# Transformer block, one core: another order of the pieces that stand beside the pairs of heads

## The reference

```python
x = x + attention(layernorm(x))      # softclamp 50*tanh(s/50), causal, softmax, projection Wo
n = layernorm(x)
shared = gelu(n @ sw1 + sb1) @ sw2 + sb2
probs = softmax(n @ gate_w + gate_b);  topk_p, topk_i = top_k(probs, 2)
routed = sum over the two chosen e: topk_p[e] * (gelu(n @ w1[e] + b1[e]) @ w2[e] + b2[e])
x = x + routed + shared
```

## Time and profile before

| | |
|---|---|
| median of 3 runs | 2223.99 us (2222.87 to 2224.55) |
| profiled execution, own time | 2222.78 us |
| its span | 2221.1 us |
| busy: TensorE, VectorE, ScalarE, GpSimd | 1953.5, 1495.0, 1419.2, 1003.5 us |
| mean granted clock of TensorE | 0.958 |
| one sequence in the steady part | 112.75 us |
| second stage, from 1835 us on | some 386 us |

### The profile page before, as it was taken

The page is one execution under the profiler, slowest core; times in us unless marked ns, Lnnn a source line. Parts: engine busy times, 40 slices in busy tenths (PEclk is TensorE's granted clock), DMA queues, the critical chain, the costliest instruction groups (busy, mean ns, idle before and its releaser), DMA issues.

```text
span 2221.1 us, 39929 instructions
## 1 busy us (share of the span) xinstructions
PE 1953.5 (88%) x14653; PEld 1525.6 (69%) x14653; DVE 1495.0 (67%) x2803; ACT 1419.2 (64%) x2170; POOL 1003.5 (45%) x1195
## 2 busy tenths in 40 slices
PE   6889898989898989898989989898989876699898
PEld 4666676766666767676666767576767654699898
DVE  5467767676767686767676767676767685566565
ACT  6768575767676766767685857676767651344444
POOL 3434545453535353535353536353535442444344
PEclk9999999999999999999999999999999987799999
DMA  3000101010101010101010101010100012665564
GB/s 123 1 10 12 38 10 39 10 39 10 39 10 39 11 39 11 39 11 39 11 39 10 39 10 39 10 39 11 39 11 30 11 39 98 211 186 173 164 183 142
DMA packets 73665, 112.51 MB, mean 51 GB/s; under 512 B 9715, under 2 KB 52218, under 8 KB 73476
## 3 DMA queue, kind: packets, MB, share of 16 engines
q1 hardware_dynamic: 58468, 67.86, 10.5%
q0 software_dynamic: 15008, 42.10, 5.1%
HBM read 63.10 MB, written 48.65 MB: 50 GB/s over the span
## 4 chain that ended last, share of the span: by engine, by line
PE 43%; DVE 28%; ACT 21%; issue 7%; DMA 1%; POOL 0%; another core or an unknown queue 0%; POOLq 0%; DVEq 0%; SPq 0%; ACTq 0%
PE ring L1188 6%; ACT prob L590 5%; ACT prob L584 5%; PE bank_o L1230 5%; DVE norm L795 4%; DVE q_lo L784 4%; PE ring L1209 3%; DVE kT L779 3%; PE ring L1195 3%; PE ring L1214 3%; ACT kT L597 2%; ACT qT L607 2%; ACT qT L601 2%; DVE oTl L809 2%; PE ring L1136 2%
## 5 line engine op out<-in xcount | busy, mean ns | idle before, releaser
L508 POOL TENSOR_SCALAR_AFFINE_SELECT prob<-prob 128x256 f32<-128x256 f32 x512 | 219.2, 443 | 683.1 <-ACT prob L590 683.0
L584 ACT ACTIVATE prob<-ring 128x1024 f32<-128x1024 f32 (+1 forms) x384 | 328.1, 877 | 269.2 <-PE ring L1214 265.1
L779 DVE TENSOR_TENSOR kT<-ring,kT 64x512 fp32r<-64x512 f32 x256 | 176.3, 688 | 414.6 <-ACT kT L597 336.6
L1230 PE MATMUL bank_o<-prob,v 128*32 128x512 f32 (+3 forms) x4096 | 327.4, 463 | 103.3 <-DVE weighed L800 85.0
L520 POOL TENSOR_TENSOR key_sum<-prob 128x768 f32<-128x768 f32 x128 | 236.5, 1848 | 261.8 <-PE bank_d L1244 252.1
L590 ACT ACTIVATE prob<-prob 128x1024 f32<-128x1024 f32 (+1 forms) x384 | 344.0, 914 | 5.2
L1230 PEld LDWEIGHTS bank_o<-prob,v 128*32 128x32 f32 x4096 | 122.0, 115 | 284.3 <-issue 188.3
L1209 PE MATMUL ring<-qT,kT 128*128 128x256 f32 (+3 forms) x1024 | 244.2, 341 | 79.5 <-ACT qT L607 23.5
L1209 PEld LDWEIGHTS ring<-qT,kT 128*128 128x128 f32 x1024 | 168.9, 192 | 156.7 <-DVE q_lo L784 37.0
L795 DVE RECIPROCAL norm<-bank_d 128x512 f32<-128x512 f32 x64 | 214.7, 3355 | 26.5 <-PE bank_d L1244 25.5
L1214 PE MATMUL ring<-q_lo,kT 128*128 128x256 f32 (+3 forms) x1024 | 229.0, 325 | 0.0
(11 more groups left out here) (224 smaller groups left out, 4665.0 us busy)
## 6 DMA issues: line engine op xcount, KB each, us to landing
xin<-first SPq DMA_DIRECT2D x71, 257.0 KB
xin<-second SPq DMA_DIRECT2D x71, 129.0 KB
xin<-base SPq DMA_DIRECT2D x71, 128.0 KB, 2.1
x_next<-in_x SPq DMA_DIRECT2D x16, 512.0 KB, 4.6
x_res<-in_x SPq DMA_DIRECT2D x16, 512.0 KB, 3.8
raw_e<-in_w SPq DMA_DIRECT2D x4, 1024.0 KB, 6.8
first<-pad SPq DMA_DIRECT2D x9, 257.0 KB, 8.7
second<-pad SPq DMA_DIRECT2D x9, 129.0 KB, 8.1
```

The source lines that it names most:

```text
L508: last = nc.gpsimd.affine_select(out=diag, in_=diag, compare_op=ALU.is_ge, fill=0.0, base=0, pattern=[[0, 2], [1, P]], channel_multiplier=-1)
L584: nc.scalar.activation(probs[p % PROBS][u][:, :, :], slot[:, :, 0:UNIT_COLS[u]], ACT.Tanh, scale=SCALE / SOFTCLAMP).then_inc(act_emptied, 1)
L779: last = nc.vector.tensor_tensor(kT[head_rows[1 - h], h, :], slot[r, 1, :], kT[r, h, :].bitcast(F32), ALU.subtract)
L1230: last = pe.matmul(bank_o[h * QD:(h + 1) * QD, j * P:N], v[:, j, f:f + QD], probs[(2 * quad + h // 2) % PROBS][u][:, h % 2, at:at + N - j ...
```

## The change

It gives pieces of a sequence other pairs to stand beside, on all engines, and computes the same.

- First layer norm of the next sequence: from pair 0 to pair 1, behind the weighing and splitting of the previous sequence's pair 7.
- Value projections: three at pair 1 and one at pair 2, instead of two and two. The output projection of the previous sequence's pair 6 goes from between the first two to behind the last one; that of pair 7 goes from pair 2 to pair 3.
- `add_attention` and the second layer norm: from pair 2 to pair 3. `turn2`: from 3 to 4. `gate`: from 4 to 5. `turn_logits`: from 4 to 5. `hidden` stays at 5, now directly behind `gate`. `choose` and `split_hidden`: from 5 to 6, behind `empty_turned1`. `count_earlier`: from the end of 6 to 7, ahead of `shared_out`.
- `empty_pos` is cut out of `place_tokens`; it stands with the rest behind `empty_qk` of pair 7, and `place_tokens` now follows `add_shared`, where it stood ahead of the weighing.
- Transfers of rows: `send_second` from pair 7 to pair 0 of the sequence after, `send_first` from pair 0 to pair 1, both behind `sum_keys`.

```diff
--- before.py
+++ after.py
@@ -90,7 +90,7 @@
             elif i + 1 < NSEQ:
                 units += [("qk", i + 1, 0, 0)]
             if i >= 1 and p in FFN_UNITS:
-                units += [(FFN_UNITS[p], i - 1, 0, 0)]
+                units += [(kind, i - 1, 0, 0) for kind in FFN_UNITS[p]]
             if i + 1 < NSEQ and p == 6:
                 units += [("turn1", i + 1, 0, 0)]
             if p in V_UNITS:
@@ -102,10 +102,10 @@
 
 
 UNIT_ORDER = (2, 0, 1)
-V_UNITS = {1: (0, 1), 2: (2, 3)}
-
-FFN_UNITS = {3: "turn2", 4: "gate", 5: "hidden", 7: "out"}
-LATE_UNITS = {4: "logits", 6: "pos"}
+V_UNITS = {1: (0, 1, 2), 2: (3,)}
+
+FFN_UNITS = {4: ("turn2",), 5: ("gate", "hidden"), 7: ("pos", "out")}
+LATE_UNITS = {5: "logits"}
 LAST_UNITS = ["turn2", "gate", "logits", "hidden", "pos", "out"]
 RING = ring_plan()
 AT = {unit: n for n, unit in enumerate(RING)}
@@ -529,12 +529,13 @@
             pool.wait_ge(const_ready, 2)
             for i in range(NSEQ):
                 for p in range(PAIRS):
+                    mask(i, p)
+                    sum_keys(i, p)
                     if p == 0 and i >= 2:
+                        send_second(i - 2)
+                    if p == 1 and i >= 2:
                         send_first(i - 2)
-                    mask(i, p)
-                    if p == PAIRS - 1 and i >= 1:
-                        send_second(i - 1)
-                    sum_keys(i, p)
+            send_second(NSEQ - 2)
             send_first(NSEQ - 2)
             pool.wait_ge(projected, NSEQ * PAIRS)
             clear_pad()
@@ -645,13 +646,13 @@
                     clamp(i, p, 0)
                     clamp(i, p, 1)
                     exponentiate(i, p, 0)
-                    if i >= 1 and p == 5:
+                    if i >= 1 and p == 6:
                         exp_gate(i - 1)
                     if p >= 3:
                         exponentiate(i, p, 1)
 
                     def meanwhile():
-                        if p == 3 and i >= 1:
+                        if p == 4 and i >= 1:
                             copy_x2_hi(i - 1)
                         if p == 6 and i + 1 < NSEQ:
                             copy_xn_hi(i + 1)
@@ -883,23 +884,25 @@
                 last.then_inc(chosen_ready, 1)
 
 
-            def place_tokens(i):
-
+            def empty_pos(i):
                 n = AT["pos", i, 0, 0]
                 slot = ring[n % 2]
-                step = [0]
-
-                def then(ins):
-                    step[0] += 1
-                    ins.then_inc(slot_steps, 1)
-                    dve.wait_ge(slot_steps, i * SLOT_STEPS + step[0])
-
                 ahead = slot[:, 0, 0:K * NT * E].rearrange("p (k t e) -> p k t e", k=K, t=NT)
                 totals = slot[:, 1, 0:K * NT * E].rearrange("p (k t e) -> p k t e", k=K, t=NT)
                 dve.wait_ge(ring_full, n + 1)
                 nc.vector.tensor_copy(place[:, :, :, :], ahead)
                 nc.vector.tensor_copy(totals_of[:, :, :, :], totals).then_inc(dve_emptied, 1)
-                dve.wait_ge(dve_emptied, EMPTIED[n][1])
+
+            def place_tokens(i):
+
+                step = [0]
+
+                def then(ins):
+                    step[0] += 1
+                    ins.then_inc(slot_steps, 1)
+                    dve.wait_ge(slot_steps, i * SLOT_STEPS + step[0])
+
+                dve.wait_ge(dve_emptied, EMPTIED[AT["pos", i, 0, 0]][1])
                 for t in range(NT):
                     then(nc.vector.tensor_tensor(taken[:, :, t + 1, :], taken[:, :, t, :], totals_of[:, :, t, :],
                                                  ALU.add))
@@ -980,11 +983,8 @@
                     chunk = (i, p - 3) if p >= 3 else (i - 1, p + 5)
                     if p == 2 or chunk[0] < 0:
                         chunk = None
-                    if i >= 1:
-                        if p == 5:
-                            empty_logits(i - 1)
-                        if p == 7:
-                            place_tokens(i - 1)
+                    if i >= 1 and p == 6:
+                        empty_logits(i - 1)
                     if i == 0 and p == 3:
                         dve.wait_ge(idle_padded, 16 * 3)
                     if chunk is not None:
@@ -1001,34 +1001,36 @@
                         split_lo(3 + p)
                         if p == 1:
                             split_lo(5)
-                    if p == 0 and i + 1 < NSEQ:
+                    if p == 1 and i >= 1:
+                        weigh_values(i - 1, PAIRS - 1)
+                        split_values(i - 1, PAIRS - 1)
+                    if p == 1 and i + 1 < NSEQ:
                         dve.wait_ge(xnext_loaded, 16 * (i + 2))
                         layernorm_stats(1, x_next)
                         layernorm_guess(1, i + 1)
                         layernorm_newton(1, i + 1)
                         layernorm_apply(1, i + 1, x_next, x_next, xn_ready)
-                    if p == 1 and i >= 1:
-                        weigh_values(i - 1, PAIRS - 1)
-                        split_values(i - 1, PAIRS - 1)
-                    if i == NSEQ - 1 and p in (3, 4, 5, 6):
-                        prepare_bias(p - 3)
+                    if p == 6 and i + 1 < NSEQ:
+                        empty_turned1(i + 1)
+                    if i == NSEQ - 1 and p in (4, 5, 6, 7):
+                        prepare_bias(p - 4)
                     if i >= 1:
-                        if p == 2:
+                        if p == 3:
                             add_attention(i - 1)
                             layernorm_guess(2, i - 1)
                             layernorm_newton(2, i - 1)
                             normalise_rows(i - 1)
-                        if p == 3:
+                        if p == 4:
                             empty_turned2(i - 1)
-                        if p == 4:
+                        if p == 5:
                             empty_gate(i - 1)
-                        if p == 5:
+                        if p == 6:
                             choose(i - 1)
                             split_hidden(i - 1)
                         if p == 7:
+                            empty_pos(i - 1)
                             add_shared(i - 1)
-                    if p == 6 and i + 1 < NSEQ:
-                        empty_turned1(i + 1)
+                            place_tokens(i - 1)
 
             last_i = NSEQ - 1
             for c in range(PAIRS - 3, PAIRS):
@@ -1043,6 +1045,7 @@
             empty_logits(last_i)
             choose(last_i)
             split_hidden(last_i)
+            empty_pos(last_i)
             place_tokens(last_i)
             add_shared(last_i)
 
@@ -1315,30 +1318,27 @@
                 pe.matmul(slot[:, 0, 0:K * NT * E], earlier[:, :], flags, start=True, stop=True)
                 pe.matmul(slot[:, 1, 0:K * NT * E], ones_r[:, :], flags, start=True, stop=True).then_inc(ring_full, 1)
 
-            FFN = {2: turn2, 3: gate, 4: hidden, 5: turn_logits, 6: shared_out, 7: count_earlier}
-
             pe.wait_ge(const_ready, 2)
             turn1(0)
             pe.wait_ge(xn_hi, 1)
             project_qk(0, 0, (lo_split, 1), (lo_split, 2))
-            MIDDLE = {3: turn2, 4: gate, 5: hidden, 7: shared_out}
-            LATE = {4: turn_logits, 6: count_earlier}
+            MIDDLE = {4: (turn2,), 5: (gate, hidden), 7: (count_earlier, shared_out)}
+            LATE = {5: turn_logits}
             for i in range(NSEQ):
                 for p in range(PAIRS):
                     for u in UNIT_ORDER:
                         scores(i, p, u)
                     if p >= 4:
                         project_out(i, p - 4)
-                    elif i >= 1 and p < 2:
+                    elif i >= 1 and p != 2:
                         project_out(i - 1, p + 4)
-                    elif i >= 1 and p == 2:
-                        project_out(i - 1, PAIRS - 1)
                     if p + 1 < PAIRS:
                         project_qk(i, p + 1)
                     elif i + 1 < NSEQ:
                         project_qk(i + 1, 0)
                     if i >= 1 and p in MIDDLE:
-                        MIDDLE[p](i - 1)
+                        for piece in MIDDLE[p]:
+                            piece(i - 1)
                     if i + 1 < NSEQ and p == 6:
                         turn1(i + 1)
                     if p == 1:
@@ -1346,13 +1346,10 @@
                             values(i - 1, PAIRS - 1)
                         else:
                             pe.wait_ge(lo_split, 3)
-                        project_v(i, 0)
-                        if i >= 1:
-                            project_out(i - 1, PAIRS - 2)
-                        project_v(i, 1)
-                    if p == 2:
-                        project_v(i, 2)
-                        project_v(i, 3)
+                    for t in V_UNITS.get(p, ()):
+                        project_v(i, t)
+                    if p == 2 and i >= 1:
```

(9 more changed lines are left out.)

## The result

The kernel after takes 2408.89 us (median of 4 runs, 2407.67 to 2412.61) against 2224.27 us before: a ratio of 1.083, with a 95% interval of 1.0815 to 1.0847. It is slower, as forecast, but by 185 us and not by 109: the time lies above the range. Its profiled execution took 2412.61 us.

The account below looks back on a forecast made before the run. TensorE was taken to set the pace at 112.75 us a sequence. Pair terms summed to 121.3, 8.55 more; 14 x 8.55 = 120, less the ends, gave +109, or 2333 us; range 2285 to 2362, eight in ten.

Parts of the forecast that it names:

- the two waits: TensorE idle before pair 3's first scores, about 6.7 us, and before `shared_out` at pair 7, some 7 us.
- the step of 5.93 us: TensorE's gap before the values of pair 7 at pair 1, forecast to go with 1.4 us of slow clock.
- the 5 to 8 us that the prediction named as their sign: Profile sign: TensorE idles this long before pair 3's first scores and before `shared_out`, both released by L784.
- its own last sign of being wrong: Prediction is wrong if the layer norm at pair 2 is as slow as GpSimd's adds can make it.
- so I take 6.0: Pair 2: 6.0 us for the first layer norm, GpSimd waiting for denominators until it is about half done.
- the upper end I had kept (8.04): Pair 2: slowest layer norm duration read before, kept for the range as +2.0 us on the 6.0.
- nearer 8: Pair 2: layer norm duration in us if small steps each wait out one GpSimd add, by the skill's rule.
- The term of 5.45: Pair 7: us for `choose` and `split_hidden` on VectorE, within the 13.6 us chain before `shared_out`.
- 3.43+1.8: Pair 7: shared output 3.43 us, plus 1.8 us for the clock after some 7 us idle.
- 11 back: First and last sequences: -4 us in sequence 0 and -7 us in the last, against 120 us added.
- costed at nothing: Row transfers behind `sum_keys`: hidden in GpSimd's waits; up to 5 us a sequence if that cover were gone.
- Rival 3: Both waits, VectorE further behind: norm 8.0, clocks 2.1 each, transfers partly uncovered; 11.5 us a sequence, about 2373 us; chance 0.07.

Follow-up runs that it names:

- two single edits: Kernel after, output projection of pair 6 back behind the first value projection: 2288.74 us; kernel after, `empty_qk` ahead of the reciprocal at pair 7: 2323.52 us.
- the norm alone: Kernel before with only the first layer norm moved from pair 0 to pair 1, behind weighing and split of pair 7: 2113.28 us.
- both edits: Kernel after with the output projection of pair 6 back and `empty_qk` ahead of the reciprocal at pair 7: 2202.75 us, ratio 0.991 to before.

## Why the prediction was right and wrong

The direction and the mechanism of the two waits held: the step of 5.93 us goes, and both new waits come at the places, by the releasers and with the causes that were named. The two single edits and their sum show them to be separate, and the norm alone shows that it was not the norm's place that was bad. Both waits are longer than the 5 to 8 us that the prediction named as their sign (8.79 and 8.49), and its own last sign of being wrong came true: the norm is as slow at its new place as GpSimd's adds can make it. Of the pairs, 0, 1, 3, 4 with 5, and 6 came within 0.3 us. `hidden` waits 1.34 us (1.5 forecast), the slot of the turned rows 0.91 (1.2), the split more than 15.

The size was wrong. In the spans, 189.8 us came where 109 were forecast; of the 81 missed, 64 lie in the 14 sequences and 17 at the ends. **Pair 2** took 23.1 us and not 20.4. The term that failed is "so I take 6.0" for the layer norm: it measured 8.52. I reasoned that GpSimd would stand still for its first half; it did, but the small steps of the second half were held up all the more, and the upper end I had kept (8.04) was too low also. The first scores unit then took 1.02 us and not 0.6, at the low clock that the sum had put into pair 3. The rule of the Trainium skill that I had put beside it, "SBUF — State Buffer", "Who interferes with whom", would have made it "nearer 8" and was the better guide: the small steps end with GpSimd's adds, and short adds bring 5.59. **Pair 7** took 23.8 and not 21.6. The term of 5.45 for `choose` and `split_hidden` measured 6.88, for the same reason: I had read it at a place where the adds had nearly ended. And `shared_out` with its slow clock took 5.84 us and not 3.43+1.8. The norm and the choice, 2.52 and 1.43 us above their terms, make 55 us in 14 sequences, most of the 64. That cutting the adds short gave 75 us, about the whole miss, is partly chance: the choice then took 4.94, less than its term, and some of the slow clock went with the shorter waits. The pairs together were 5.0 us short, the forecast difference only 4.6, because its base of 112.75 was itself 0.4 below the mean sequence of 113.16.

**The ends** were wrong by 17 us. Sequence 0 and the last were to give 11 back; by the spans they took some 6 more (189.8 against 184). They are still the first stage: TensorE starts on the experts' rows at 1905.91 us before and 2092.92 after, not at 1835, so 187.0 us of the difference lie ahead of the second stage. In sequence 0 the waits of 5.0 and of 3.6 us at the value projections went, but one of 7.9 came for `empty_qk`, because the norm now stands behind VectorE's preparation of weights, which waits for ScalarE. In the last sequence the 3.2 us for GpSimd's sums went, but TensorE waited 10.1 us for `choose`, 7.8 for the turned rows and 5.8 for the weighing, where it had waited 7.2, 6.5 and 4.4 before. All three stand behind `prepare_bias` in VectorE's order, and I had taken it to be no dearer than before. These two causes are read from the timelines and the order of the code and were not tried.

**The transfers** were costed at nothing, with GpSimd's queue looked at for lateness alone. In the kernel before with the norm moved they cost 27 us: 1.3 of idle in a sequence and, every other time, 1.6 of slow clock. Whether they cost anything in the kernel after was not tried by itself; there the split of pair 7 takes 1.35 us (998.69 to 1000.04), so little of that cost lies in it.

Rival 3 (both waits, VectorE further behind, 2373) came nearest, and its price was still 36 us short. Its chance of 0.07 was too low: I had seen the norm at 8.04 and at 5.56 and decided by an argument on overlap where the overlap of each small step could have been laid out.

## What to carry to other kernels

Where two engines hold each other up, price a moved stretch of small instructions by what the other engine runs at the new place, and a moved piece of that other engine by whom it lets run sooner: a transfer that costs nothing itself can be the spacer that keeps two engines apart. In an order written by hand, a wait inside a stretch holds up all that stands behind it on its engine; ask for each moved producer which consumer now waits early, and what follows it. In a ring of two slots, look at the second piece behind a slow one.

## What the runs showed of the hardware

GpSimd's adds lengthen some of VectorE's instructions that overlap them: one of 0.16 us took 1.81 beside an add of 1.80 (1053.61), and the layer norm took 8.52 us where it took 5.59 with the adds cut short. Others they leave alone: the reciprocal at 994.59 took 3.34 us beside two adds, and 3.36 elsewhere. GpSimd's issues of indirect transfers hardly do: beside them (0.98 us each) the split took 1.32 us, beside the adds 2.64, and 1.15 with neither.

An idle time of under 2 us was sometimes enough for TensorE's lower clock. With the output projection of pair 6 back, the same wait of 1.92 us stands in 15 sequences; behind it the values took 4.05 us in seven of them (granted clock 0.57 from 990.5 to 994.5) and 2.36 in the others. With both edits the same wait left them at 2.36 in 13 of 15 sequences. With the transfers moved, behind waits of 1.68 us, six stretches of half clock lie between 250 and 1600 us, where the norm alone had none. What decides between the two cases is not shown.

The low clock costs more behind a longer wait. Behind 5.93 us the values took 3.69 us for 2.36. Before `shared_out` the clock was already 0.50 inside the wait (998.0 to 1002.9) and stayed there for what came next, which took 5.84 us for 3.43.
